# One phase takes a turned operand that an earlier phase kept, and moves its value product behind the output projection

## What is computed

```python
def block0(x, context):
    x = attn(ln(x, g1, b1), ln(x, g1, b1), Wq1, Wk1, Wv1, Wo1, bo1) + x   # SELF:  16 heads of 64
    x = attn(ln(x, g2, b2), context, Wq2, Wk2, Wv2, Wo2, bo2) + x         # CROSS: 16 heads of 64
    return geglu(ln(x, g3, b3), Wp, bp, Wf, bf) + x                       # GEGLU

def block1(x, xf):
    q, k, v = x @ Wq + bq, xf @ Wk + bk, xf @ Wv + bv                     # CROSS2: 16 heads of 8
    out = softmax(q * 8 ** -0.5 @ k.T) @ v @ Wo + bo                      # per batch and head
    h = gelu(ln(out) @ W1 + b1)                                           # FFN
    return x + out + (h @ W2 + b2)

y = block1(block0(x, ctx_768), ctx_768)
```

## Time and profile before

| | |
|---|---|
| median of 3 runs | 463.67 us (463.36 to 463.86) |
| the profiled execution | 463.25 us, its span from first to last instruction 461.5 us |
| granted TensorE clock, mean | 1.000 (of 2.4 GHz) |
| PE busy | 446.6 us (97%) |
| PEld busy | 407.7 us (88%) |
| DVE, ACT, POOL busy | 351.7, 326.3, 199.2 us |

### The profile page before, as it was taken

One profiled execution on the slowest core, in us unless ns is written; L12 is line 12 of the kernel. 1 busy time (PEld: TensorE's weight loads), 2 busy tenths in 40 slices (PEclk: granted clock), 3 DMA queues, 4 the chain that ended last, 5 costly groups with the idle time before them and its releaser, 6 DMA issues.

```text
span 461.5 us, 17534 instructions
## 1 busy us (share of the span) xinstructions
PE 446.6 (97%) x7574; PEld 407.7 (88%) x7574; DVE 351.7 (76%) x641; ACT 326.3 (71%) x599; POOL 199.2 (43%) x219
## 2 busy tenths in 40 slices
PE   7989999999999999999999999999999999999897
PEld 6979899898998998989989899898999787777797
DVE  4898779678797786887967869786884778889572
ACT  4686777877878768777787777855545576776773
POOL 2585333555454535543354333531532232132583
DMA  7102020310200000000000000000000000000011
GB/s 226 37 20 83 4 81 3 77 47 4 61 4 12 1 13 10 3 11 4 10 12 1 13 10 3 4 1 3 1 0 10 18 10 20 0 2 1 9 38 48
DMA packets 17301, 10.57 MB, mean 23 GB/s; under 512 B 7888, under 2 KB 16272, under 8 KB 17232
## 3 DMA queue, kind: packets, MB, share of 16 engines
q1 hardware_dynamic: 16800, 9.48, 7.4%
q10 hardware_dynamic: 432, 0.07, 0.1%
HBM read 8.50 MB, written 1.05 MB: 21 GB/s over the span
## 4 chain that ended last, share of the span: by engine, by line
PE 86%; DVE 8%; ACT 3%; issue 1%; POOL 1%; DMA 1%; DVEq 0%; POOLq 0%; ACTq 0%
PE stage L605 12%; PE stage L606 11%; PE stage L607 11%; PE scp L696 7%; PE scp L771 7%; PE scp L917 6%; PE scp L741 6%; PE out0p L791 4%; PE out0p L817 3%; PE out0p L792 3%; PE out0p L793 3%; PE stage L755 2%; PE scp L712 2%; PE stage L620 1%; PE stage L835 1%
## 5 line engine op out<-in xcount | busy, mean ns | idle before, releaser
L1455 POOL TENSOR_TENSOR pr<-pr,rc 128x1024 f32<-128x1024 f32 x32 | 60.3, 1905 | 70.1 <-DVE rc L1248 70.1
L1003 ACT ACTIVATE pr<-pr 128x1024 f32<-128x1024 f32 x48 | 50.7, 1056 | 32.5 <-DVE pr L1218 24.6
L1396 POOL TENSOR_TENSOR rstd<-veps,neghalf 128x2 f32<-128x2 f32 x32 | 22.4, 701 | 86.5 <-DVE veps L1166 86.4
L1255 DVE COPY vt<-stage 64x512 f32<-64x512 f32 x47 | 32.5, 694 | 31.1 <-PE stage L607 30.1
L941 ACT ACTIVATE vt<-stage 64x512 f32<-64x512 f32 x81 | 48.0, 592 | 4.7 <-PE stage L607 1.2
L1261 DVE TENSOR_TENSOR ot_r<-scp,ot_h 128x512 fp32r<-128x512 f32 x64 | 41.0, 684 | 10.4 <-ACT ot_h L941 10.4
L941 ACT ACTIVATE q_of_heads<-stage 128x512 f32<-128x512 f32 x62 | 35.3, 596 | 10.3 <-PE stage L607 8.5
L1213 DVE TENSOR_REDUCE mx<-scp 128x16 f32<-128x1024 f32 x32 | 39.2, 1225 | 4.4 <-PE scp L696 3.6
L941 ACT ACTIVATE k_of_heads<-stage 128x512 f32<-128x512 f32 x62 | 37.1, 600 | 5.4 <-PE stage L607 0.3
L1246 DVE TENSOR_REDUCE sm<-pr 128x16 f32<-128x1024 f32 x32 | 38.8, 1212 | 2.6 <-ACT pr L1003 2.6
L1218 DVE TENSOR_TENSOR pr<-scp,mx 128x1024 f32<-128x1024 f32 x32 | 39.2, 1225 | 1.1
(11 more groups left out here) (254 smaller groups left out, 1407.0 us busy)
## 6 DMA issues: line engine op xcount, KB each, us to landing
ctx_in<-in_ctx_dram SPq DMA_DIRECT2D x16, 96.0 KB, 2.0
masked_k<-in_L_xattn_Wo_dram SPq DMA_DIRECT2D x2, 512.0 KB, 3.8
out_dram<-rows SPq DMA_DIRECT2D x8, 128.0 KB, 1.8
rows<-in_x_dram SPq DMA_DIRECT2D x1, 768.0 KB, 9.5
pr<-in_L_xattn_Wq_dram SPq DMA_DIRECT2D x1, 512.0 KB, 4.4
pr<-in_L_xattn_Wk_dram SPq DMA_DIRECT2D x1, 512.0 KB, 6.2
pt<-in_L_xattn_Wv_dram SPq DMA_DIRECT2D x1, 512.0 KB, 7.7
rows<-in_L_xattn_Wq_dram SPq DMA_DIRECT2D x1, 512.0 KB, 3.8
```

The lines of the kernel that those rows point to most:

```text
L1003: nc.scalar.activation(pr[t][:, :], pr[t][:, :], ACT.Exp, scale=scale[s.phase]).then_inc(exped, 1)
L1455: nc.gpsimd.tensor_tensor(halves(pr[t][:, :]), halves(pr[t][:, :]), rc[:, t, :, None].to_broadcast([ROWS, H, N]), ALU.mult).then_inc(probs, 1)
```

## The change

CROSS writes its turned context tile no longer into `cT`, of which there were two, but into a place of its own for each group, in the first 96 partitions of `rows2` (256 columns a group). CROSS2 reads q, k and v's context operand from there. So CROSS2 loads no context, turns none and copies none, and the buffer `cT` is gone. The output of CROSS2 for a group overwrites the same 256 columns of `rows2` after they were read. The groups of CROSS2 are written out on all engines, with no loop. On PE the v product of group s+1 moves from behind `cross2_out_step(before, 1)` to behind `wo_step(before)`, in front of the scores of group s+1; on DVE its copy into `vb` moves from in front of the second max to the end of the group.

```diff
         if p != CROSS2:
             self.tick("high", (p, g))
             self.tick("rest", (p, g))
-        if p in WITH_CTX:
+        if p == CROSS:
             self.tick(f"ctx{g % 2}", (p, g), 16)
             self.tick("ctx_turned", (p, g))
...
-                if p in (SELF, CROSS):
+                if p in (SELF, CROSS, CROSS2):
                     for g in range(GROUPS):
                         body(Step(p, g))
                     continue
...
+        def turned_ctx(s):
+
+            return rows2[0:C, s.first * GR:(s.first + 1) * GR]
...
-            for p in WITH_CTX:
+            for g in range(2):
+                load_ctx(Step(CROSS, g))
+            with sp.Fori(0, GROUPS // 2 - 1) as turn:
                 for g in range(2):
...
-                if s.phase in WITH_CTX:
+                if s.phase == CROSS:
                     pe.wait_ge(ctx_loaded[s.parity], cnt.at(f"ctx{s.parity}", s))
                     for t in range(T):
...
-                nc.tensor.matmul(bank[:, GR:2 * GR], wk1[:, :], cT[s.parity][:, :], start=True, stop=True)\
+                nc.tensor.matmul(bank[:, GR:2 * GR], wk1[:, :], turned_ctx(s), start=True, stop=True)\
...
-                                                cT[s.parity][:, b * N:(b + 1) * N],
+                                                turned_ctx(s)[:, b * N:(b + 1) * N],
                                                 wv1_by_parity[:, e, :, :], start=True, stop=True)
...
                     if before:
                         cross2_out_step(before, 1)
-                    if not last:
-                        v_step(one, s)
-                        if two.phase == CROSS2:
-                            x_step(two, s)
+                    if two.phase == CROSS2:
+                        x_step(two, s)
                     cross2_turn_step(s, 0)
...
                     if before:
                         wo_step(before, s)
                     if not last:
+                        v_step(one, s)
                         cross2_scores_step(one, s)
...
-                if s.phase in WITH_CTX:
-                    last = copy(cT[s.parity][:, :], bank[0:C, GR:2 * GR])
+                if s.phase == CROSS:
+                    last = copy(turned_ctx(s), bank[0:C, GR:2 * GR])
...
                     if before:
                         cross2_norm_step(before)
-                    if not last:
-                        p_step(one)
                     cross2_max_step(s, 1)
                     cross2_shift_step(s, 1, before)
                     if two.phase == FFN:
                         norm_step(two, one)
                     if before:
                         wo_step(before)
-                    if last:
+                    if not last:
+                        p_step(one)
+                    else:
```

More of the change, by code:

```diff
@@ L41 @@
 WARM_UP = 9
-WITH_CTX = (CROSS, CROSS2)
 def proj_by_dve(p, g):
@@ L186, in group @@
                 self.qk(p, g + 1)
-                self.use("v", p, g + 1)
                 if two.phase == CROSS2:
@@ L197, in group @@
                 self.use("wo", p, g - 1)
-            if not last and two.phase == FFN:
-                self.x(two.phase, two.first)
+            if not last:
+                self.use("v", p, g + 1)
+                if two.phase == FFN:
+                    self.x(two.phase, two.first)
             for name in ("out0", "norm", "atted"):
@@ L298, in attention_blocks @@
         xT = [sb(f"xT{n}", [D, GR]) for n in range(2)]
-        cT = [sb(f"cT{n}", [C, GR]) for n in range(2)]
         src = [[sb(f"src{n}{m}", [D, GR], F32R) for m in "hr"] for n in range(2)]
@@ L416, in each_group @@
                     continue
[L417 to L420, removed]
+                tail = 4 if looks_far else 2
+                turns = (GROUPS - tail) // 2
                 with eng.Fori(0, turns) as turn:
-                    body(Step(p, lead, turn, turns))
-                    body(Step(p, lead + 1, turn, turns))
+                    body(Step(p, 0, turn, turns))
+                    body(Step(p, 1, turn, turns))
                 for g in range(GROUPS - tail, GROUPS):
@@ L540, in load_ctx @@
                              c[:, bass.ds(step.at(T), T), :]).then_inc(ctx_loaded[step.parity], 16)
-            for p in WITH_CTX:
+            for g in range(2):
+                load_ctx(Step(CROSS, g))
+            with sp.Fori(0, GROUPS // 2 - 1) as turn:
                 for g in range(2):
[L544 to L550, removed]
+                    sp.wait_ge(ctx_turned, cnt.at("ctx_turned", Step(CROSS, g, turn, GROUPS // 2 - 1)))
+                    load_ctx(Step(CROSS, g + 2, turn, GROUPS // 2 - 1))
             o = out.rearrange("b n d -> (b n) d").rearrange("(t p) d -> p t d", p=ROWS)
@@ L968, in x_high_step @@
                 if s.phase == CROSS:
-                    last = copy(ctx_src[s.parity][0][:, :], cT[s.parity][:, :])
+                    last = copy(ctx_src[s.parity][0][:, :], turned_ctx(s))
                 last.then_inc(high, 1)
@@ L1425, in rest_step @@
                     hp, rp = ctx_src[s.parity]
-                    last = nc.gpsimd.tensor_tensor(rp[:, :], cT[s.parity][:, :], hp.bitcast(F32)[:, :], ALU.subtract)
+                    last = nc.gpsimd.tensor_tensor(rp[:, :], turned_ctx(s), hp.bitcast(F32)[:, :], ALU.subtract)
                 last.then_inc(rest, 1)
```

## The result

The changed kernel takes 469.74 us (median of 4 runs, 469.18 to 471.08) where the kernel before takes 463.65 (4 runs, 463.36 to 463.86): 1.0134 times as long, 95% interval 1.0122 to 1.0146. The direction was forecast, the time lies 0.5 us above the range. The profiled execution took 470.11 us, its span is 468.4 us, 6.9 more than before.

A forecast was written before the change was run, and what follows sets the result against it. In CROSS2 the path scores, max, shift, exponential was taken to bound the first turn, not PE's work. Terms -0.26 + 0.60 + 2.10 + 0.60 + 0.50 + 0.20 = +3.74 us gave 467.4 on the median of 463.67, range 465.3 to 469.2.

The forecast's parts named there:

- start of group 0's scores: End of GEGLU: one pair of context transposes leaves PE's path, -0.26 us (bounds 0 and -0.52).
- group 0: CROSS2 group 0: PE already waits for the exponential, so v behind the projection adds +0.60 us.
- groups 1 to 5: CROSS2: each group 8.78 us for 8.36, v's 0.60 partly repaid by the bank wait; +2.10 us (bounds 1.8 and 3.0).
- group 6: CROSS2 group 6: v adds +0.60 us without repayment, DVE's copies delaying statistics and max add +0.50 (0.3 to 0.8).
- from group 7's scores to the end: Group 7's max comes 0.31 us later, some of it reaching the end: +0.20 us (bounds 0 and 0.31).
- the mechanism: CROSS2: the first turn waits for the exponential, 0.14 us behind its end; context work gains 0 there, moved v costs 0.60.
- the clock: PE in CROSS2: clock stays at 2.4 GHz, 0 in the sum; at 1.2 GHz up to 19 us more over five groups.
- nothing outside 350 to 434 us: Rest of the kernel: no change of time counted outside 350 to 434 us; one there was a sign of being wrong.
- PE as the bound: Rival for CROSS2: PE's work sets the pace, groups of 7.92 us, total 461.2 us; chance 0.07.
- Less than it says: Rival: the exponential comes 0.4 us earlier, five groups keep 8.36 us, statistics hide; 464.6 us; chance 0.08.
- Late copies of v: Rival: v reaches DVE 0.3 to 0.5 us later, five groups lose 0.1 to 0.3 each; 467.9 to 468.9; chance 0.12.
- The fall of the clock: Rival: PE's clock falls in CROSS2 after the new waits, priced at 19 us over five groups; chance 0.02.

The follow-up runs named there:

- e11: The changed kernel itself run once more, nothing altered: 467.79 us, 1.0100 of the kernel before.
- e2: The kernel before with only the v product and its copy moved; context work and loop stay: 469.78 us, 1.0120 of the kernel before.
- e5: The kernel before with only groups 2 to 5 of CROSS2 written out on all engines: 464.32 us, 1.0006 of the kernel before.
- e8: The changed kernel with the context loads of CROSS issued 9 to 10 us later: 468.63 us, 1.0093 of the kernel before.
- e1: The changed kernel with the v product and its copy put back in their old place: 463.68 us, 1.0001 of the kernel before.
- e7: The changed kernel with v made earlier, right behind q and k, its copy before the division, three vb buffers: 462.19 us, 0.9965 of the kernel before.
- e13: Second single profile of e3's kernel (changed kernel, group 6 kept warm): 468.95 us at clock 0.996.
- e3: The changed kernel with five idle matmuls in front of group 6's first turn: 467.16 us, 1.0104 of the kernel before.
- e4: The changed kernel with FFN's statistics on DVE behind the first shift in groups 6 and 7: 466.54 us, 1.0073 of the kernel before.
- e12: First single profile of e3's kernel (changed kernel, group 6 kept warm): 466.49 us at clock 1.00.
- e9: e7 (v early) with the context loads of CROSS issued later as well: 462.35 us, 0.9969 of the kernel before.
- e10: e3 with 8 more idle matmuls in front of group 0's first turn: 467.42 us, 1.0078 of the kernel before.

## Why the prediction was wrong

e11's profiled execution kept its clock (467.14 us, span 465.4), so the sum can be checked with and without the fall. Its scores start at 358.83, 366.66, 376.50, 385.18, 393.86, 402.54, 411.22 and 420.72 us.

| term, us | forecast | profiled run of the change | e11, clock 1.00 |
|---|---|---|---|
| start of group 0's scores | −0.26 | +0.70 | +0.33 |
| group 0 | +0.60 | +0.51 | +0.51 |
| groups 1 to 5 | +2.10 | +1.67 | +1.66 |
| group 6 | +1.10 | +2.88 | +1.15 |
| from group 7's scores to the end | +0.20 | +1.14 | +0.25 |
| sum | +3.74 | +6.90 | +3.90 |

**Right, the mechanism.** The first turn waits for the exponential, 0.14 or 0.15 us behind its end in the groups 1 to 6 and 0.05 in group 0, so the removed context work gave nothing and v behind the projection cost time. Its signs are there, two of them just under their range: groups 8.68 us apart (8.7 to 8.9 forecast), idle time in front of the first turn released by ACT (0.55, where 0.6 to 0.9 was forecast), no wait inside the turn, v 0.62. DVE's first max starts at S+1.22 in the ordinary groups and at S+2.07 in group 6 (1.95 forecast). Group 6 takes 9.50 us at full clock (9.3 to 9.6 forecast). The forecast of 8.78 was 0.10 too long: 0.03 in front of the turn and 0.07 behind it, 3.71 for 3.78.

**Right in part by luck, the size.** The 0.32 us of an ordinary group, for 0.42 forecast, are not all v's: e2, with v alone, has 0.19, and e5 0.07 for the writing out, which the sum put at 0. That the sum at full clock, +3.90, comes so close to +3.74 is due to two misses that cancel, 0.44 too much in the groups 1 to 5 and 0.59 too little at the start. One reading is wrong, with nothing resting on it: DVE's busy time in group 5 is 6.86 us, the 6.69 is PEld's.

**Wrong, the step "the clock".** The prediction said that PE already stood idle for 0.59 us in group 6 with the clock at 1.00, "so the sum has 0 for it". That compared the old wait with the old clock. The new waits follow from the prediction's own terms: in group 6 0.59, plus 0.60 of v gone, plus 0.50 from the late statistics, 1.69 us (measured 1.74); in group 0 0.35, plus 0.60 of v and 0.26 of context, 1.21 us (measured 1.32). Neither sum was made, and the price of the fall was worked out for five ordinary groups, which keep the clock in every profile. The kernel before held a hint: PE runs 5 idle matmuls (`keep_warm`; the trace has two records for each) in front of the first turn of group 0, in the wait that the change lengthens.

```profile
361.71 1.29 PE L600 MATMUL stage<-ident 128*128 128x128 f32 x10
```

In the profiled execution the fall cost 2.88 − 1.15 in group 6 and 1.14 − 0.25 behind it, 2.62 us; all four runs behind the median had a fall. What the runs show in place of that 0 is a loss of clock at the long waits, 2.62 us in this execution, in some executions and not in others; a granted clock below 1.00 was among the prediction's own signs of being wrong. Executions of the changed kernel or of e8 with clock 1.00 took 466.65 to 467.64 us, around the predicted 467.4. The rule that was weighed there, the Trainium skill (TensorE: Matmul & The Clock Gate, Part 1: The HAM clock gate), that an idle PE falls back to 1.2 GHz, decided it. The trace agrees in the fall itself, with 0.50 behind a wait of 1.74 us; this idle time is shorter than the one that section gives for a fall, and here the measurement decides.

**Wrong but small, "nothing outside 350 to 434 us".** In the profiled run PE came 0.91 us later to the end of GEGLU, 0.76 of it in the stall of CROSS, and the context transposes there gave back 0.21 (0.26 forecast): +0.70. In e11 it came 0.54 us later, 0.27 of it in the stall: +0.33. Most of the rest arose ahead of the stall, in code that the change leaves alone, and was not traced.

**The rivals.** PE as the bound would have made groups of 7.92 us: refuted by 8.68, and by e1 beside e5, where less PE work gives no time back. The Trainium skill (Perfetto Trace Analysis, Identifying Performance Opportunities) points to the engine with the highest occupancy, but says that for TensorE the busy share of matmuls is no good measure and that of the weight loads is one. By that, PE has 6.69 us in group 5 and DVE 6.86, so the rule did not plainly name PE, as the prediction took it to; PE at 98% was not what to relieve. "Less than it says" is refuted: 1.66 us more in the groups 1 to 5 instead of none. Late copies of v are refuted: they end at S+0.97, before the max could start at S+1.22. The fall of the clock, given 0.02, came true, at the two long waits rather than in five groups.

## What to carry to other kernels

Work that fills a wait costs nothing but the waits that it causes itself, and taking it out gains no more than these; moved behind the thing waited for, it is paid, less what these waits took (here 0.60 us of work cost 0.51 in group 0 and 0.35 in group 1). Before taking it out, add up the wait that remains, in the worst group and with everything else that becomes late there, and compare that length with the longest wait at which this kernel has been seen to keep its clock; a clock that held at the old, shorter wait says nothing about the new one. If the operand can be made earlier, move the work to the front of the wait, and look for the bank that it frees and the engine that it relieves (e7).

## What the runs showed of the chip that was not expected

- One wait of 1.32 or 1.74 us between stretches of busy PE is enough for the granted clock to halve: for some 3.4 us in e13, 7 in the changed kernel and in e8, 10 in e2. In three of these profiles it falls while PE is already busy again, in e2 just before the turn. It does not do so each time: of 22 executions of kernels with both waits (the change, e2, e8, e11; in e2 the first is 1.10) 15 show it, of 14 with the first and a shorter one in group 6, 0.34 or 0.92 (e3, e4, e12, e13), 5, of 38 in which no wait in front of a first turn is longer than 0.57 (e1, e5, e7, e9, e10) none. It is not quite unknown there either: the kernel before, with 0.59, has 1 execution among the 47 beside the experiments that lost its clock (465.98 us at 0.996, beside e5); where, no profile shows.
- 5 idle matmuls in group 6's wait took 1.38 us and delayed nothing, because the wait was longer (first turn at S+5.70 in e3, S+5.79 in e11); in all four profiles with them (e3, e10, e12, e13) the clock stayed at 1.00 in group 6. With 13 in group 0's it stayed at 1.00 too (e10), but they delayed the turn by 0.29 us.
- PE can stand still for 0.53 to 1.29 us inside a row of equal matmuls for no reason that the profile shows (CROSS, at 239 to 240 us in every profile); the length differs between executions.
